# Graph attention in one kernel: the weighting of gathered rows moved from bursts to one per slot, seven quads behind

## The reference, cut to what matters

```
score = sum(q_dst * k_src)                        # layer 3: a code of the edge times h_dst, plus a term of the source
m     = segment_max(score, dst)
e     = exp(score - m[dst])
out   = segment_sum(value_src * e, dst) / segment_sum(e, dst)
```

## Time and profile before

| what | us |
|---|---|
| runs of the kernel before, lowest, median, highest | 5542.47, 5544.4, 5549.68 |
| span of the profiled execution, first to last instruction | 6456.7 |
| span over the median | 912.3 |
| stretches of the four rounds of attention in the profile, together | 3388 |

### The profile page before, as it was taken

The page is one execution under the profiler, slowest core; times in us unless marked ns, Lnnn a source line. Parts: engine busy times, 40 slices in busy tenths (PEclk is TensorE's granted clock), DMA queues, the critical chain, the costliest instruction groups (busy, mean ns, idle before and its releaser), DMA issues. The chain is left out here.

```text
span 6456.7 us, 68859 instructions
## 1 busy us (share of the span) xinstructions
PE 4457.4 (69%) x19341; PEld 3493.0 (54%) x19341; DVE 3832.0 (59%) x8692; ACT 1605.5 (25%) x3882; POOL 3364.1 (52%) x3108
## 2 busy tenths in 40 slices
PE   5666664577766666778857767796766679766776
PEld 4455453444436455557845555685555558545554
DVE  7544443544455666675347766643766776567777
ACT  3433332200004111113421211243211214312221
POOL 2588886366644555541356555134555530256663
PEclk9888887788888778779977777898778779878887
DMA  3688887255556555542266556315556541256664
GB/s 139 121 124 125 121 125 150 81 184 184 182 165 208 168 173 181 181 144 58 81 189 182 174 175 181 89 56 165 169 175 182 176 147 39 80 168 183 195 192 134
DMA packets 508435, 959.75 MB, mean 149 GB/s; under 512 B 85846, under 2 KB 298020, under 8 KB 507251
## 3 DMA queue, kind: packets, MB, share of 16 engines
q0 software_dynamic: 224512, 549.90, 34.1%
q1 hardware_dynamic: 283426, 404.92, 19.6%
q10 hardware_dynamic: 128, 0.52, 0.0%
HBM read 718.56 MB, written 236.50 MB: 148 GB/s over the span
## 5 line engine op out<-in xcount | busy, mean ns | idle before, releaser
L1460 POOL DMA_INDIRECT L2a_rows<-kv_rows,typed_index x960 | 966.3, 1007 | 627.8 <-DVE L2a_weighted L1615 349.9
L1765 PE MATMUL L2a_sums<-L2a_weighted,L2a_hot 128*128 128x264 f32 x2784 | 830.5, 450 | 166.8 <-DVE L2a_weighted L1615 159.4
L1754 PE MATMUL L2a_query<-x,L2a_turned 128*128 x2784 | 819.8, 447 | 55.8 <-ACT L2a_turned L1709 33.0
L867 POOL DMA_INDIRECT sum_rows<-L0s_rows,L0s_row_of x464 | 724.6, 1562 | 152.9 <-issue 119.4
L1765 PEld LDWEIGHTS L2a_sums<-L2a_weighted,L2a_hot 128*128 128x128 f32 x2784 | 591.2, 221 | 314.5 <-DVE L2a_weighted L1615 186.2
L1754 PEld LDWEIGHTS L2a_query<-x,L2a_turned 128*128 128x128 f32 x2784 | 627.2, 229 | 181.4 <-issue 62.5
L1460 POOL DMA_INDIRECT hold<-kv_rows,typed_index x432 | 445.4, 1031 | 449.8 <-DVE L2a_weighted L1615 279.5
L1460 POOL DMA_INDIRECT L3a_rows<-feature_rows,index x464 | 489.1, 1054 | 301.7 <-DVE L3a_weighted L1615 155.1
L1285 POOL DMA_INDIRECT L1s_rows<-rows,index x464 | 451.0, 972 | 351.2 <-issue 133.8
L1717 ACT ACTIVATE L2a_hot<-L2a_hot 128x512 f32<-128x512 uint8 x348 | 218.7, 629 | 1470.8 <-PE L2a_sums L1765 726.6
L1002 PE MATMUL L0s_message<-features,L0s_share 128*128 x928 | 312.8, 496 | 285.9 <-ACT L0s_share L967 285.9
(11 more groups left out here) (428 smaller groups left out, 8550.9 us busy)
## 6 DMA issues: line engine op xcount, KB each, us to landing
code_rows<-L1s_code SPq DMA_DIRECT2D x116, 512.0 KB
L3a_code<-code_rows SPq DMA_DIRECT2D x116, 512.0 KB
L0s_wide<-source_rows SPq DMA_DIRECT2D x116, 256.0 KB
L2a_turn<-turned_rows SPq DMA_DIRECT2D x87, 256.0 KB
L2a_pens<-mask_rows SPq DMA_DIRECT2D x87, 256.0 KB
L2a_hot<-hot_rows SPq DMA_DIRECT2D x87, 256.0 KB
kv_rows<-L2d_key_rows SPq DMA_DIRECT2D x50, 384.0 KB, 2.6
kv_rows<-L2d_value_rows SPq DMA_DIRECT2D x150, 128.0 KB, 2.4
```

Source lines behind the costliest of these rows:

```text
L867: pool.indirect_dma_start(c.sum_rows[u], bass.IndirectOffsetOnAxis(ap=row_of[:, 4 * n + u:4 * n + u + 1], axis=0), rows[n % ring][:, u, :] ...
L1460: pool.indirect_dma_start(rows[n % ring][:, u, :], None, table, bass.IndirectOffsetOnAxis(ap=index_of[:, t:t + 1], axis=0)).then_inc(lande ...
L1754: last = pe.matmul(query[q % 2][:, u, :], turned[quad % 2][:, u, :], at(c.q, b[2 * q + u // 2]), start=True, stop=True)
L1765: last = pe.matmul(sums[(m * WP + j) % held][:, :], hot[quad % 2][:, j % 2 * 2 + k, :], weighted[:, 2 * j + k, :], start=k == 0, stop=k == 1)
```

## The change

The whole of `attend` becomes a pipeline of slots, one per quad g. In each slot VectorE weighs quad g - 7, then multiplies quad g, runs the part of the chain that is due, reduces quad g, and adds the two sums of quad g - 8; in the fourth slot of a group product and reduce come first and back to back. There are now 31 iterations (`WG + 2`) and not 30. The ring is 12 quads in layer 2 and 13 in layer 3. `weighted` becomes three buffers of a quad, `score` and a new `prob` are doubled, `prods` becomes single, and the correction factor is copied to SBUF (`shrink`). ScalarE gets four small copies per group (`column`, the probabilities into every 33rd column of `weighted`) and one (`keep_shrink`). On TensorE each small product stands ahead of the query matmuls of its slot. Cut to its core:

```diff
-    held, codes = 3, 4
+    held, codes, late, kept, quads = 3, 4, 2 * WQ - 1, 3, WG * WQ
-        ring = RQ if typed else 11
+        ring = 12 if typed else 13
-        weighted = st.sb("weighted", [P, WT, VC])
-        prods = [st.sb(f"prods{k}", [P, 4, D]) for k in range(2)]
-        score = st.sb("score", [P, WT, H])
+        weighted = [st.sb(f"weighted{k}", [P, 4, VC]) for k in range(kept)]
+        prods = st.sb("prods", [P, 4, D])
+        score = [st.sb(f"score{k}", [P, WT, H]) for k in range(2)]
+        prob = [st.sb(f"prob{k}", [P, WT, H]) for k in range(2)]
+        shrink = st.sb("shrink", [P, H])
...
             load_turn(0)
-            for n in range(WG):
-                load_codes(n)
-                if n + 1 < WG:
-                    load_turn(n + 1)
-                load_pens(n)
-                load_hot(n)
+            for g in range(codes - 1):
+                load_code(g)
+            load_turn(1)
+            for n in range(WG + 1):
+                load_code(n * WQ + 3)
+                load_pens(n)
+                load_code(n * WQ + 4)
+                load_hot(n - 1)
+                load_code(n * WQ + 5)
+                load_turn(n + 2)
+                load_code(n * WQ + 6)
...
+            def product(g):
+                if g < quads:
+                    wait(dve, query_ready, g + 1)
+                    wait(dve, score_ready if typed else summed, g)
...
+            def add(w, k, b):
+                if 0 <= w < quads:
+                    j = 2 * w + k
+                    wait(dve, sums_ready, j + 1)
+                    wait(dve, added, j)
+                    if w % WQ == 0 and k == 0:
+                        wait(dve, rescaled, w // WQ)
...
+            def weigh(w):
+                if 0 <= w < quads:
+                    q = w % WQ
+                    wait(dve, prob_ready, w // WQ + 1)
+                    wait(dve, sums_ready, 2 * (w - kept + 1))
...
+            for n in range(WG + 2):
+                m, g = n - 1, n * WQ
+                weigh(g - late)
+                product(g)
+                if chain:
+                    scan_up(m)
+                    scan_down(m)
+                    spread_ends(m)
+                reduce(g)
+                rescale(n - 2, blocks[0])
+                add(g - late - 1, 0, blocks[0])
+                add(g - late - 1, 1, blocks[1])
+                weigh(g + 1 - late)
+                product(g + 1)
+                if chain:
+                    chain_up(m)
+                    chain_down(m)
+                    grow(m)
+                reduce(g + 1)
+                add(g - late, 0, blocks[2])
+                add(g - late, 1, blocks[3])
+                weigh(g + 2 - late)
+                product(g + 2)
+                if chain:
+                    pick_own(m)
+                    join_own(m)
+                    reach_first(m)
+                    reach_last(m)
+                    spread_fall(m)
+                    lower(m)
+                reduce(g + 2)
+                add(g + 1 - late, 0, blocks[4])
+                add(g + 1 - late, 1, blocks[5])
+                product(g + 3)
+                reduce(g + 3)
+                weigh(g + 3 - late)
+                add(g + 2 - late, 0, blocks[6])
+                add(g + 2 - late, 1, blocks[7])
...
+            def keep_shrink(m):
+                if 0 < m < WG:
+                    wait(act, shrink_ready, m)
+                    wait(act, rescaled, m - 1)
+                    act.activation(shrink[:, :], shrink_ps, ACT.Copy).then_inc(shrink_kept, 1)
+            def column(w):
+                if 0 <= w < quads:
+                    q = w % WQ
+                    wait(act, prob_ready, w // WQ + 1)
+                    wait(act, sums_ready, 2 * (w - kept + 1))
+                    act.activation(weighted[w % kept][:, :, HD::HC], prob[w // WQ % 2][:, 4 * q:4 * q + 4, :], ACT.Copy
+                                   ).then_inc(column_ready, 1)
+            for n in range(WG + 2):
+                m, g = n - 1, n * WQ
+                for s in range(WQ):
+                    widen(g + s - late + 1)
+                    turn(g + s + 3)
+                    if s == 1:
+                        drop(m)
+                    if s == 2:
+                        soften(m)
+                        keep_shrink(m)
+                    column(g + s - late + 1)
...
+                total(g - late, 0)
+                sequence(m)
+                ask(g + 2, near[0], near[1])
+                total(g - late, 1)
+                total(g + 1 - late, 0)
+                expand(m)
+                ask(g + 3, near[2], near[3])
+                total(g + 1 - late, 1)
+                total(g + 2 - late, 0)
+                unflatten(m)
+                ask(g + 4, near[4], near[5])
+                total(g + 2 - late, 1)
+                ask(g + 5, near[6], near[7])
+                flatten(n)
+                total(g + 3 - late, 0)
+                total(g + 3 - late, 1)
```

More of the change, by code:

```diff
@@ L1527, in join @@
-            def join(n, q):
-                if not typed:
-                    quad = n * WQ + q
-                    own = score[:, 4 * q:4 * q + 4, :]
-                    wait(dve, landed[quad % ring], 64 * (quad // ring + 1))
-                    wait(dve, summed, quad + 1)
-                    dve.tensor_tensor(own, own, rows[quad % ring][:, :, D:D + H], ALU.add).then_inc(joined, 1)
-                    if q == WQ - 1:
-                        wait(dve, joined, quad + 1)
-                        flat = score[:, :, :].rearrange("p u h -> p (u h)")
-                        dve.scalar_tensor_tensor(flat, flat, 0.2, flat, ALU.mult, ALU.max).then_inc(score_ready, 1)
@@ L1628, in _ @@
             dve.memset(c.acc[:, :, :], 0.0)
-            for n in range(WG + 1):
-                m = n - 1
-                more, chain, tail = n < WG, m >= 0, m >= 1
-                if chain:
-                    blocks = load_blocks(nc, mybir.EngineType.DVE, c, max(m - 1, 0) * WP, 2 * WP if tail else WP)
-                    before, now = blocks[0:WP], blocks[-WP:]
-                if more:
-                    product(n, 0)
+            for n in range(WG + 2):
+                m, g = n - 1, n * WQ
+                chain = 0 <= m < WG
+                if n >= 2:
+                    blocks = load_blocks(nc, mybir.EngineType.DVE, c, (n - 2) * WP, WP)
+                else:
+                    blocks = [0] * WP
+                weigh(g - late)
+                product(g)
@@ L1638, in _ @@
                 if chain:
                     scan_up(m)
-                if tail:
-                    add(m - 1, 3, before[3])
-                if chain:
                     scan_down(m)
-                if more:
-                    reduce(n, 0)
-                if chain:
                     spread_ends(m)
-                if tail:
-                    add(m - 1, 4, before[4])
-                if more:
-                    join(n, 0)
-                    product(n, 1)
+                reduce(g)
@@ L1674, in _ @@
                     lower(m)
-                if more:
-                    product(n, 2)
-                if tail:
-                    add(m - 1, 7, before[7])
-                if chain:
-                    weigh(m, 0)
-                    rescale(m, now[0])
-                if more:
-                    reduce(n, 2)
-                if chain:
-                    weigh(m, 1)
-                    add(m, 0, now[0])
-                if more:
-                    product(n, 3)
-                    join(n, 2)
@@ L1690, in _ @@
-                if chain:
-                    weigh(m, 2)
-                    add(m, 1, now[1])
-                if more:
-                    reduce(n, 3)
-                    join(n, 3)
-                if chain:
-                    weigh(m, 3)
-                    add(m, 2, now[2])
-            for j in range(3, WP):
-                add(WG - 1, j, now[j])
+                reduce(g + 2)
+                add(g + 1 - late, 0, blocks[4])
+                add(g + 1 - late, 1, blocks[5])
+                product(g + 3)
@@ L1718, in widen @@
                                    hot8[m % 2][:, q * 4 * P:(q + 1) * 4 * P], ACT.Copy).then_inc(hot_ready, 1)
             def drop(m):
-                if m >= 1:
+                if 0 < m < WG:
                     wait(act, gap_ready, m)
@@ new lines, in total @@
+            def total(w, k):
+                if 0 <= w < quads:
+                    j = 2 * w + k
+                    wait(pe, weighted_ready, w + 1)
+                    wait(pe, column_ready, w + 1)
+                    wait(pe, hot_ready, w + 1)
+                    wait(pe, added, j - held + 1)
+                    for u in range(2):
+                        last = pe.matmul(sums[j % held][:, :], hot[w % 2][:, 2 * k + u, :],
+                                         weighted[w % kept][:, 2 * k + u, :], start=u == 0, stop=u == 1)
```

288 lines of the change are left out of this document (115 added, 173 removed).

## The result

The changed kernel takes 5678.15 us in the median of four runs (5677.45 to 5685.32), the kernel before beside it 5547.04 (5542.47 to 5551.92, four runs). The ratio is 1.0237, 95% interval 1.0222 to 1.0251: 131 us slower, where 5552 and a range of 5425 to 5640 were forecast. The profiled execution of the changed kernel spans 5677.1 us, so it stands for the runs.

What follows compares the result with a forecast made beforehand. The prediction took GpSimd's gathers to pace the kernel, 21.0 us per group in layer 2 and 21.7 in layer 3. Pairs in layer 3 (6 us) and round ends (2 us) gave 5544.4 + 8 = 5552 us, range 5425 to 5640.

Steps and rivals of the forecast that it cites:

- Part 2: VectorE's order: ten new dependent pairs at 0.13 us, 1.3 us per group; hidden in layer 2, 6 us in layer 3.
- Part 7: Registers: VectorE's sequencer loads 8 block numbers per group instead of 16, priced at 0.
- the cover of 21.0: GpSimd's gather time per group in layer 2, 21.0 us, under which VectorE's 20.7 us was to stay hidden.
- Part 1: Gathers: same number and tables, so 21.0 and 21.7 us per group stay; priced at 0.
- the 912 us: Profiled span above the runs' median: put down mostly to TensorE's results seen late during gathers, going with the recording.
- Rival A: Waits for TensorE at `chain_up` and `pick_own` are partly real and go: 58 to 209 us less, 5444 us; chance 0.32.
- parts 4, 5 and 6: New waits, priced 0; ScalarE's five small copies, at most 2.0 us per group, hidden; SyncE's loads in another order, priced 0.
- part 8: End of a round: more quads left to weigh and add, 24.1 us against 23.7, +2 us for four rounds.
- rival D: The longer pipeline lies bare at each end of a round: +23 us, 5567 us; chance 0.10.
- Rival C: The ring was short, GpSimd idles behind weighings; even release and two more buffers win 23 us, 5521 us; chance 0.04.
- Rival B: VectorE paces and pays 151 us for ten pairs, if a gather's pitch is under 1.21 us: 5695 us; chance 0.12.

Runs made afterwards that it cites:

- e4: Kernel before with three gathers per quad instead of four and three pairs of adds put back to back: 6004.26 us against 6428.46 for the kernel before.
- e6: Changed kernel with three gathers per quad instead of four once the ring has been filled once: 5903.17 us against 6421.46 for the kernel before.
- e3b: Changed kernel with paired adds and chain operations parted, layer 3's join moved, block numbers loaded after the first weighing: 5617.74 us, ratio 1.0119 to the kernel before.
- e8: Same order as e3b, weighing reads the probabilities from a PSUM bank taken from sums: 6776.61 us against 6478.38 for the kernel before.
- e9: Changed kernel, order untouched, weighing reads the probabilities from a PSUM bank taken from sums: 6520.77 us against 6478.38 for the kernel before.
- e10: Kernel before, order untouched, weighing reads the probabilities from a PSUM bank taken from sums: 7228.50 us against 6478.38 for the kernel before.
- e8b: Same kernel as e8, run again: 5495.61 us, ratio 0.9893 to the kernel before.
- e1: Changed kernel with the second add of each slot moved so that no two adds stand back to back: 6260.97 us against 6421.46 for the kernel before.
- e2: Changed kernel with adds left in pairs but scan and chain operations parted by other operations: 6250.42 us against 6421.46 for the kernel before.
- e7: Changed kernel itself, run again without an edit: 5687.98 us, ratio 1.0245 to the kernel before.
- e11b: Same kernel as e11, run again: 5995.20 us against 6428.46 for the kernel before.
- e10b: Same kernel as e10, run again: 5655.18 us, ratio 1.0188 to the kernel before.
- e11: Same order as e3b with three gathers per quad instead of four: 6053.40 us against 6478.38 for the kernel before.
- e5: Kernel before with three gathers per quad instead of four from the ring's second pass on: 5405.29 us against 5552.43 for the kernel before.
- e1b: Same edit as e1, run again: 5654.75 us, ratio 1.0185 to the kernel before.

## Why the prediction was wrong

**Part 2, the price of a pair, is the step that failed.** It took 0.13 us for each of ten pairs from the one pair that the rows showed, `pick_own` to `join_own`. For five pairs that was right: 0.10 to 0.13 for scan, ends, `chain_down`, `grow`, and product 3 with its reduce. The four second adds cost 0.30 each and the one behind `rescale` 0.2. Together 2.0 us and not 1.3. e4 shows the 0.30 by itself. These five dearer pairs are the ones whose second operation has its address from a register; whether that makes the price no run parted.

**Part 7, the registers, failed with it.** Eight numbers instead of sixteen were priced at 0 because the old order hides the load. It costs 0.39 us per group behind a pair of adds. VectorE's own cycle is then 19.3 + 2.0 + 0.4 = 21.7 us, as measured in e6, and not 20.7: past the cover of 21.0, where every tenth counts. In layer 3 the step gave 21.9 and the runs 23.6; besides the same two terms, `join` behind its reduce costs 0.2 us in each of three more places and 0.1 more for the add behind it, as the timeline of layer 3 has it (1.30 and 0.22 us of pitch, where 1.13 and 0.10 stood before):

```profile
5309.92 1.20 DVE L1530 TENSOR_REDUCE L3a_score<-L3a_prods 128x32 f32<-128x1024 f32 x1
5311.22 0.19 DVE L1538 TENSOR_TENSOR L3a_score<-L3a_score,L3a_rows 128x32 f32<-128x32 f32 x1
5311.44 0.43 DVE L1552 TENSOR_TENSOR acc<-acc,L3a_sums 128x264 f32 x1
```

That makes 20.1 + 2.0 + 0.4 + 0.9 = 23.4 us; the last 0.2 is not accounted for.

**Part 1, the gathers at 0, was wrong as well.** What of the loss is whose? The part took the gathers' 1.015 us for a constant; they rose by 0.04 us each in layer 2, because more of them started early in a weighing. In layer 3 GpSimd even waits for weighings and the 53 us are VectorE's. In layer 2 the 63 us are VectorE's by e6, but e3b shows that with the pairs parted GpSimd holds the group at 21.5 us, so they were lost twice over. The Trainium skill (SBUF — State Buffer, Who interferes with whom and SBUF: two separate sides) says that a VectorE instruction with two SBUF inputs contends with a GpSimd instruction that reads SBUF, and that the first one holds the port for its whole length. The traces agree on which operations collide: a gather reads its offsets from SBUF, a weighing read two operands there, and in the traces of e8, e9, e10 and e8b, where one of the two moved to PSUM, not one gather that starts within a weighing is lengthened; products, with one operand in PSUM all along, lengthen nothing. They differ on the length: in the timeline above a gather that has run 0.16 us no longer blocks a weighing, nor is it blocked. By that rule the weighings were a suspect from the start; the prediction didn't weigh it.

**The reading of the 912 us was wrong in kind.** They don't go with the recording. Rival A took the waits at `chain_up` and `pick_own` for partly real, and in executions of the long kind they are: there e1 and e2, the changed kernel with small edits, are 2.7% faster than the kernel before. In the short kind they are absent, and A had nothing to win. The changed kernel itself ran in no long set, so how it stands there isn't known. What makes a set long isn't either: the chip recorded as number 8 had a short set (e7) and a long one (e11b) within the hour.

**What held.** GpSimd paces before; 19.4 and 20.2 us are VectorE's own cycles; parts 4, 5 and 6 (new waits, ScalarE, loads) cost nothing that shows; part 8's small price for the ends, +2 us (its terms add to 24.0, not 24.1, and its bound takes three more weighings where it counts two), stands beside about 5 us by which the ends of the four rounds grew, and not the 23 of rival D. Rival C had nothing to win: in the second profile of before GpSimd waits for no weighing. Rival B named the mechanism, VectorE pays for the pairs, and 5695 us is near. But it tied it to a condition that isn't met (a gather's pitch under 1.21 us; it is 1.31), and its chance of 0.12 was set by that condition. Its 151 us for ten pairs at 0.13 is near the measured 131 by luck: it counts from 19.4 to 20.7 us, both VectorE's, where the runs went from GpSimd's 20.9 to VectorE's 21.7. It was the price of the pairs that decided, and not B's condition. The signs were in the forecast: 20.7 against a cover of 21.0, and 21.9 against 21.7, were sums from a single measured pair, and a doubling of that one price would have turned them.

## What to carry to other kernels

Where two engines have nearly the same cycle, a term of a tenth of a microsecond decides, and relieving one of them can show next to nothing, as in layer 2 of e3b: take both causes away in one run before you call either harmless. Don't stand two operations back to back when the second waits for the first, least of all ahead of a register load; the dearest pairs here, 0.30 us each, were adds with an address from a register, and one large operation between them hid all of it. Look at the operands of every VectorE operation that runs beside indirect gathers, and try one of two SBUF operands in PSUM; count what the bank costs, since the same edit won in one order (e8b) and lost in another (e10b). Before you argue from a profile whose span is far above the median, take a second one.

## What the runs showed that wasn't expected

- The same kernel takes 5543 to 5565 us in some sets and 6417 to 6493 in others, steady within a set. In the long kind VectorE resumes late after TensorE's small products, by over 6 us. Every kernel with three gathers per quad is 424 to 518 us faster than the kernel before there (e6 5903, e11b 5995, e4 6004, e11 6053), where e5 gained 147 in a short set; so fewer gathers go with less of that lateness, but they don't end it.
- The order of the kernels isn't the same in the two kinds. e8 and e8b are one kernel: 4.8% slower than before in a long set, 1.1% faster in a short one. e1 and e2: 2.7% faster in the long, 1.9 and 2.6% slower in the short.
- With both operands of the weighing in SBUF, a gather that starts during it ends 0.82 us after its end, whether it began 0.1 or 1.0 us into it (2.0 to 0.95 us long); elsewhere it takes 0.95 us. Of 81 weighings in 450 us of e1b, 49 had a gather start within them that took over 1.2 us.
